# Attention scores as plain fp32 products in the two row halves of TensorE, without the split of q and k

## The reference

```python
# layer 0
xn = group_norm(x)                                   # 32 groups
q, k, v = split(qkv_w @ xn + qkv_b)                  # per head: 64 x 2304 each
x = proj_w @ (softmax(q^T k / 8) v) + proj_b + x
# layer 1: q and k come from x joined with a table of positions, v from x
q, k, v = [x, emb] @ Wq, [x, emb] @ Wk, x @ Wv
x = (softmax(q k^T / 8) v) @ Wout + bout + x
```

## Time and profile before

| | |
|---|---|
| median of 3 runs | 4401.74 us |
| the profiled execution | 4398.31 us |
| its span | 4396.5 us |
| attention of layer 0, layer 1 | about 420 to 2080 us, 2603 to 4265 us |
| TensorE, VectorE, ScalarE, GpSimd busy | 94%, 78%, 63%, 41% of the span |
| granted clock of TensorE, mean | 0.99 |

### The profile page before, as it was taken

How to read it: one execution, slowest core, us unless ns; L and a number is a source line. 1 busy time by engine, 2 the same in 40 slices (tenths; PEclk the granted TensorE clock), 3 DMA queues, 4 the chain that set the end, 5 groups by cost and what they waited for, 6 DMA issues and landing times. The chain is left out here.

```text
span 4396.5 us, 84946 instructions
## 1 busy us (share of the span) xinstructions
PE 4117.0 (94%) x29976; PEld 2458.3 (56%) x29976; DVE 3426.9 (78%) x3564; ACT 2790.3 (63%) x2981; POOL 1802.6 (41%) x584
## 2 busy tenths in 40 slices
PE   7998899999999999998999979999999999999989
PEld 4554555555555555554555545555555555555545
DVE  4222899999999999998433339999999999999972
ACT  1111788888888888886001027888888888888840
POOL 0000455555555555555100005555555555555540
PEclk9999999999999999999999999999999999999999
DMA  4334111212112111120444441212112111111216
GB/s 191 136 127 142 31 49 39 61 35 55 43 49 51 38 50 44 47 68 32 157 144 162 139 133 24 61 35 59 38 50 55 38 48 39 52 41 50 61 43 208
DMA packets 234733, 321.67 MB, mean 73 GB/s; under 512 B 12081, under 2 KB 221105, under 8 KB 233649
## 3 DMA queue, kind: packets, MB, share of 16 engines
q1 hardware_dynamic: 214512, 292.54, 23.0%
q10 hardware_dynamic: 20160, 28.32, 1.8%
HBM read 188.69 MB, written 132.12 MB: 73 GB/s over the span
## 5 line engine op out<-in xcount | busy, mean ns | idle before, releaser
L617 POOL TENSOR_TENSOR prob<-prob,mx 128x1344 f32<-128x1344 f32 x576 | 1781.6, 3093 | 2433.0 <-DVE two_tiles L894 1445.0
L772 ACT ACTIVATE prob<-psum_att 128x1152 f32<-128x1152 f32 x1152 | 1290.4, 1133 | 597.6 <-DVE run L874 336.4
L706 PE MATMUL psum_att<-qst,kst 128*128 128x384 f32 x6912 | 1420.2, 349 | 48.7 <-DMA kst<-qk_scratch 27.9
L785 ACT ACTIVATE prob<-prob 128x1152 f32<-128x1152 f32 x1152 | 1299.2, 1166 | 37.5 <-POOL prob L617 37.5
L706 PEld LDWEIGHTS psum_att<-qst,kst 128*128 128x128 f32 x6912 | 1177.1, 190 | 185.6 <-ACT prob L772 91.4
L719 PE MATMUL psum_att<-prob,vst 128*32 128x384 f32 x13824 | 1237.5, 491 | 34.6 <-ACT pvr L791 29.3
L617 DVE TENSOR_TENSOR prob<-prob,mx 128x960 f32<-128x960 f32 x576 | 974.1, 1691 | 173.0 <-ACT mx L779 173.0
L874 DVE TENSOR_TENSOR run<-psum_att,run 128x1152 f32<-128x1152 f32 x768 | 1004.3, 1347 | 13.0 <-PE psum_att L706 12.8
L719 PEld LDWEIGHTS psum_att<-prob,vst 128*32 128x32 f32 x13824 | 399.5, 109 | 625.1 <-issue 594.7
L894 DVE TENSOR_TENSOR two_tiles<-prob 128x768 f32<-128x768 f32 x576 | 565.9, 983 | 0.0
L314 PE MATMUL psum<-xc_l,wq 128*128 128x384 f32 x1536 | 504.3, 490 | 11.0 <-DVE hl_l L419 5.8
(11 more groups left out here) (59 smaller groups left out, 1906.7 us busy)
## 6 DMA issues: line engine op xcount, KB each, us to landing
qk_scratch<-hl_l SPq DMA_DIRECT2D x48, 1536.0 KB, 5.6
qst<-qk_scratch SPq DMA_DIRECT2D x192, 384.0 KB, 5.6
kst<-qk_scratch SPq DMA_DIRECT2D x192, 192.0 KB, 3.3
v_scratch<-vo_l SPq DMA_DIRECT2D x24, 768.0 KB, 3.5
vst<-v_scratch SPq DMA_DIRECT2D x96, 192.0 KB, 2.5
att_scratch<-ob ACTq DMA_DIRECT2D x96, 192.0 KB, 1.9
attc_l<-att_scratch SPq DMA_DIRECT2D x24, 768.0 KB, 5.5
x_sb<-in_x SPq DMA_DIRECT2D x8, 1152.0 KB, 14.1
```

The lines of the kernel that those rows point to most:

```text
L617: return engine.tensor_tensor(x, x, m, ALU.subtract)
L706: mm = nc.tensor.matmul(psum[:, 3 * e + k, 0:CH], kst[:, e, (3 * c + k) * P:(3 * c + k + 1) * P], qst[par][:, 2 * w + e, :], start=(w == 0 ...
L772: nc.scalar.activation(chunk_of(par, c, e), s_bank(e), ACT.Copy).then_inc(copied, 1)
L785: nc.scalar.activation(x, x, ACT.Exp, scale=SCALE).then_inc(exp_done, 1)
```

## The change

- `qkv_stage` makes no high and low part: ScalarE (layer 0, L360) or VectorE (layer 1, with the table) writes q and k once, in fp32. `qk_scratch` has one plane.
- A score tile is one fp32 product per head over 64 rows, head 0 in rows 0 to 63 and head 1 in rows 64 to 127 of TensorE, into two banks.
- A slot is one key tile for both heads (two banks, 128x768), three slots per chunk. `copy` and `maximum` work on slots: 18 and 16 per block, in place of 12 and 10 of 128x1152. The exponential is one of 128x2304 per chunk. All folds are one maximum of 128x768.
- The transposes of both heads stand together ahead of the chunk's scores. `turn_den` becomes three small products with a 128x2 matrix `heads`, which also drops the reduction L904. `reduce` and `norm` become three each, one per bank pair.
- SHIFT_DVE goes from 160 to 208. VectorE pairs before it shifts, and GpSimd waits for VectorE's shift of the same chunk instead of for a pair.
- q and k are loaded by one transfer per block, and one per chunk of keys.

```diff
-SHIFT_DVE = 160
+SHIFT_DVE = 208
...
-                        sp.dma_start(qkv["qk"].rearrange("m w p t -> p (m w) t")[:, half * MT:(half + 1) * MT, tokens(i)],
-                                     hl[half].rearrange("p m w t -> p (m w) t")).then_inc(stored, 16)
+                        sp.dma_start(qkv["qk"].rearrange("m p t -> p m t")[:, half * CT:(half + 1) * CT, tokens(i)],
+                                     qk[half][:, :, :]).then_inc(stored, 16)
...
-                            nc.vector.tensor_tensor(low, bufs["sum"][m % 2][:, :], high, ALU.subtract)\
-                                .then_inc(low_done, 1)
...
+                            nc.vector.tensor_tensor(qk[half][:, mt, :], qk_bank(m), emb_of(i, m), ALU.add)\
+                                .then_inc(qk_out, 1)
...
             def turn_den(t):
                 pe.wait_ge(den_copied, t + 1)
                 for r in range(3):
-                    mm = nc.tensor.transpose(spare_bank(0, r), den[:, r * P:(r + 1) * P], ident)
+                    mm = nc.tensor.matmul(psum[:, 5, CH + 2 * r:CH + 2 * r + 2], den[:, r * P:(r + 1) * P], heads,
+                                          start=True, stop=True)
...
+            def scores(t, par, c, k):
+                if c == 0 and k == 0:
+                    pe.wait_ge(q_in[par], 16 * (t // 2 + 1))
+                if k == 0:
+                    pe.wait_ge(k_in[c], 16 * (t // JB + 1))
+                for e in range(2):
+                    rows = slice(e * D, (e + 1) * D)
+                    mm = nc.tensor.matmul(psum[:, 2 * k + e, 0:CH], kst[rows, (3 * c + k) * P:(3 * c + k + 1) * P],
+                                          qst[par][rows, :], start=True, stop=True, tile_position=(e * D, 0))
                 mm.then_inc(scored, 1)
...
             def body(t, par):
                 for c in range(KC):
...
+                    spare_free(t, c)
+                    if c == TURN_AT and not before(t, 1) and live(t - 1):
+                        bank_free(t, c, 2)
+                        turn(t - 1)
+                    if c == BROADCAST_AT and not before(t, 1) and live(t - 1):
+                        bank_free(t, c, 2)
+                        broadcast_max(t - 1)
...
+                    if live(t):
+                        for k in range(3):
+                            bank_free(t, c, k)
+                            scores(t, par, c, k)
...
-                nc.scalar.activation(chunk_of(par, c, e), s_bank(e), ACT.Copy).then_inc(copied, 1)
+                nc.scalar.activation(prob[par][:, :, s, :], s_banks(k)[:, :, 0:CH], ACT.Copy).then_inc(copied, 1)
...
-                nc.vector.tensor_tensor(r[:, :, :], s_bank(e), other, ALU.max).then_inc(maxed, 1)
+                nc.vector.tensor_tensor(r[:, :, :], s_banks(s % 3)[:, :, 0:CH], other, ALU.max).then_inc(maxed, 1)
...
                         pool.wait_ge(copied, slot(t, 3 * c + 2))
-                        pool.wait_ge(paired, group(t, c))
+                        pool.wait_ge(dve_shifted, group(t, c))
                         shift_part(nc.gpsimd, par, c, SHIFT_DVE, CH).then_inc(pool_shifted, 1)
```

More of the change, by code:

```diff
@@ L6 @@
 F32 = mybir.dt.float32
-F32R = mybir.dt.float32r
 ALU = mybir.AluOpType
@@ L675, in turn @@
[L675 to L684 removed]
+                    pe.wait_ge(mx_ready, t)
@@ new lines, in spare_free, with turn @@
+                if c == DEN_TURN_AT + 1 and not before(t, 3) and live(t - 3):
+                    pe.wait_ge(inverted, t - 2)
+                if c == DEN_SPREAD_AT + 1 and not before(t, 3) and live(t - 3):
+                    pe.wait_ge(normed, 3 * (t - 2))
+            def turn(t):
+                pe.wait_ge(folded, t + 1)
+                for e in range(2):
+                    for r in range(3):
+                        mm = nc.tensor.transpose(psum[:, 2 * r + e, CH:512], fold[:, e, r * P:(r + 1) * P], ident)
+                mm.then_inc(turned, 1)
@@ L736, in body @@
                 for c in range(KC):
[L737 to L748 removed]
+                    spare_free(t, c)
[5 more added lines that the diff above has]
+                        broadcast_max(t - 1)
+                    if c == DEN_TURN_AT and not before(t, 3) and live(t - 3):
+                        bank_free(t, c, 2)
+                        turn_den(t - 3)
+                    if c == DEN_SPREAD_AT and not before(t, 3) and live(t - 3):
+                        bank_free(t, c, 2)
+                        spread_den(t - 3)
+                    if live(t):
+                        for k in range(3):
+                            bank_free(t, c, k)
+                            scores(t, par, c, k)
                     tv, pv, cv = behind(t, par, c, PV_LAG)
@@ L863, in maximum @@
-            def maximum(t, par, c, e):
-                r = run[e]
-                dve.wait_ge(scored, scored_count(slot(t, c, e)))
-                if c == 1:
-                    dve.wait_ge(copied, slot(t, 0, e))
+                    dve.wait_ge(broadcast, t)
+                nc.vector.tensor_reduce(mcol[:, :, r], s_banks(r)[:, :, CH:512], AX.X, ALU.max).then_inc(reduced, 1)
+            def maximum(t, par, s):
+                r = run[s % 2]
+                dve.wait_ge(scored, scored_count(slot(t, s)))
+                if s < 4:
+                    dve.wait_ge(copied, slot(t, s - 2))
@@ L884, in shift @@
-            def shift(t, par, c):
-                if c == 0:
-                    dve.wait_ge(mx_ready, unit(t, 1))
-                dve.wait_ge(copied, slot(t, c, 1))
-                shift_part(nc.vector, par, c, 0, SHIFT_DVE).then_inc(dve_shifted, 1)
+                    dve.wait_ge(turned, t)
+                nc.vector.tensor_tensor(fold[:, :, :], run[0][:, :, :], run[1][:, :, :], ALU.max).then_inc(folded, 1)
             def pair_tiles(t, par, c):
-                dve.wait_ge(exp_done, slot(t, c, 1))
+                dve.wait_ge(exp_done, group(t, c))
@@ L895, in pair_tiles, with shift @@
                                         prob[par][:, :, 3 * c + 1, :], ALU.add).then_inc(paired, 1)
+            def shift(t, par, c):
+                if c == 0:
+                    dve.wait_ge(mx_ready, t + 1)
+                dve.wait_ge(copied, slot(t, 3 * c + 2))
+                shift_part(nc.vector, par, c, 0, SHIFT_DVE).then_inc(dve_shifted, 1)
             def invert(t):
```

302 lines of the change are left out of this document (119 added, 183 removed).

## The result

The kernel after takes 4349.5 us (median of four runs, 4348.8 to 4350.6) against 4401.4 for the kernel before: a ratio of 0.9883, 95% interval 0.9866 to 0.9901. It is faster by 52 us where I forecast 131. The profiled execution has a span of 4347.7 us.

A forecast was written before the change was run, and what follows sets the result against it. TensorE and VectorE were both near their limit, so the chain between them set the block: 33.8 to 32.5 us over 96 blocks saves 125, the starts 6, 4398 to 4267 profiled, 4270 median; range 4185 to 4430.

The forecast's parts named there:

- maxima and fold of c=5 to 32.4. I take 32.5: End of the chain of a block: VectorE's fold done at 32.4 us, taken as 32.5 because some handoffs are missed.
- First tile to its reader, 0.90: Chain at c=1: broadcast and two tiling changes done at 6.3 us, first tile's maximum at 7.2.
- Chunk 2.06, tiling change 0.1: TensorE: a chunk's scores take 1.96 us, 2.06 with the change of tiling; a change costs about 0.1.
- Rival 3: Tiling changes cost up to 0.34 us for 0.1, eight on the chain: 34.1 a block, 4425 us; chance 0.07.
- `turn_den` 1.15: TensorE: three small fp32 products, six instructions at 0.19 us, 1.15 in all, +0.85 a block; alternatives 0.6 and 1.7.
- stays covered: ScalarE: 25 us a block and 1.5 of small work, below 33, so it does not set the pace.
- rival 1: TensorE's scores: row halves do not overlap, twelve rounds a chunk, 11.8 us more a block, 5360 us; chance 0.12.
- Rival 2: TensorE's scores: row halves overlap in part, seven rounds for six, 33.8 us a block, 4390 us; chance 0.08.
- The sums of work: Work per block after the change: TensorE 32.0 us, VectorE 29.9 us plus 0.6 behind GpSimd at c=0.
- VectorE idle ahead of every first maximum: Named sign that the forecast is wrong: VectorE waiting before the first maximum of every chunk.
- Outside the blocks: 3 us each start.: TensorE's two 14 us waits for the first k shrink by 3 us each, bounds 0 and 7.
- dropping it gives nothing more: `qkv_stage`: the split on ScalarE and VectorE lies under TensorE's products, so dropping it saves no further time.

The follow-up runs named there:

- e8: Kernel after with its new slots, order, shift split and `turn_den`, but before's fp32r products, high and low parts and transfers: 4353.3 us, ratio 0.9894.
- e12: e8 with the three edits of e7 and the exponential of c=3 put ahead of that chunk's copies: 4262.3 us, ratio 0.9688.
- e1: Kernel after with ScalarE's copy of `pvr` moved ahead of the exponential of c=3: 4335.5 us, ratio 0.9852.
- e7: Kernel after with e1's edit, the maxima copied before the last slot of c=1, and `turn_den` between second and third tile of c=2: 4294.3 us, ratio 0.9760.
- e4: Kernel after with a chunk's six score products issued as three of head 0, then three of head 1: 5078.9 us, a single run.
- e5: Kernel after with SHIFT_DVE back at 160, so GpSimd shifts 1344 elements again: 4359.6 us, ratio 0.9908.

## Why the prediction was right and wrong

**The step that failed** is "maxima and fold of c=5 to 32.4. I take 32.5": I walked one chain, and allowed 0.1 for all missed handoffs. The block is 33.56 (the mean of two neighbours). The 4349.5 lies inside the range that I gave, but that is luck: up there the range stood on a `turn_den` of 1.7 and dearer changes of tiling, and `turn_den` came out cheap. By its own milestones (us from the end of the fold, forecast and measured): scores 0.8 and 0.93; first maximum of c=1 7.2 and 7.70; maxima copied 11.35 and 12.05; first maximum of c=2 13.55 and 13.96; first normalization 18.7 and 19.37; first maximum of c=5 28.95 and 29.88; fold 32.4 and 33.56. It grows in small terms:

- *First tile to its reader, 0.90.* Measured 1.12 and 1.06 (1240.91 to 1242.03, 1247.23 to 1248.29) and 1.11 at c=3 (1252.59 to 1253.70). The 0.2 is paid at c=1 to c=3: 0.6 in all, the largest term. I had two rounds of 0.33 and 0.25 for the handoff. The first round of a chunk takes 0.42, and from the end of both rounds to the reader it is 0.3 to 0.4.
- *Chunk 2.06, tiling change 0.1.* Measured 2.13, and 0.14 to 0.18 for each change from transposes to row halves (by the lines of e8 and e12, which have no such change there). The Trainium skill ("TensorEngine Tiling (Array Packing)", Key Properties) only says that a change drains the engine; the drain is real and cost more than the 0.1 that the earlier trace rows gave for another pair of tilings. Rival 3 is thus half right: not 0.2 more on eight changes, but some 0.06 on four, and that sufficed, with the rest, to undo the form's gain.
- *`turn_den` 1.15.* Measured 0.73 to 0.76 with the change, which I had at 0.1 more: 0.5 too dear. Without this error the forecast would have been further off.
- *A wait not listed.* I let `weigh` go on without asking what stands ahead of `pvr`'s copy on ScalarE. The exponential of both halves in one instruction does (2.12 us); VectorE then stands 0.24 at c=5. ScalarE "stays covered" was right of its sum and wrong of its order. e1 shows 14 us for it.
- *Tails.* The third `reduce` is 0.22 late; three maxima and the fold 0.2 longer than priced.

e1 and e7 show that a part of this could be given back by order alone: with ScalarE's two copies moved and `turn_den` behind the second tile the block is 32.96, and with the exponential moved 32.88, near the 32.5 that I forecast for the order as it was.

**Right, and confirmed.** The row halves run side by side, in rounds of 0.32 (rival 1 falls; e4 shows what happens otherwise). Rival 2 falls too: the chunk has six rounds, 2.13, and not the 2.55 that I had estimated from four row tiles at 3.07 times in the Trainium skill ("TensorE: Matmul & The Clock Gate", Part 3); two row tiles on other banks cost the time of one. The sums of work: TensorE 32.0 against 32.2 busy, VectorE 29.9 and 0.6 behind GpSimd against 30.8. The first is in part luck, since `turn_den` was priced too high and chunks and changes of tiling too low. In the blocks no shift takes above 1.46, where the earlier trace rows had 3.32, and one pair, at c=0, is blocked: 1.18 for 0.95, so 0.23 where I had 0.6. The Trainium skill ("SBUF — State Buffer", SBUF: two separate sides) describes the shared pair as held for a whole instruction, and e5 agrees: the pair of 1.51 ends one free pair after GpSimd ends. VectorE's idle at the maxima copy, forecast 0.75, is 0.80. Of the signs that I named for being right, the chunk was near (2.13 for 2.06) and only the block of 32.5 was not there. But one sign of being wrong was nearly there, and it points at the step that failed: VectorE idle ahead of every first maximum. In the lines of after it waits for TensorE's first tile at c=1 (0.75), c=2 (0.45), c=3 (0.42) and c=5 (0.24).

**"Outside the blocks: 3 us each start."** Measured 34 us in all. The starts gave 4.8 and 5.1, inside their bounds of 0 to 7. I left out the fill and the drain of each layer, where no other block covers a stage: they gave 9.2 and 8.3 us. e8 has the same, so they come with the new layout; of the drain's 8.3, 5 go with the new shift split (e5). That the fill's part comes from slots of one key tile is likely but not shown alone, and the next three blocks took 1.6 us of it back. And "dropping it gives nothing more" failed: before, TensorE waited 3.59 us for the second image's statistics on VectorE, which made low parts between them; e8, which makes low parts too, has the same 3.59, and after does not wait. TensorE before and after at that place:

```profile
83.44 0.59 PE L81 MATMUL psum<-gn_mv,const_sb 128*128 128x4 f32 x2 [3.59 <-DVE gn_mv L74]
```

```profile
79.36 0.28 PE L78 MATMUL psum<-gn_mv,const_sb 128*128 128x4 f32 x2
```

The earlier trace rows shows this line at the start of the kernel, held for 19.07 us by the same releaser; I read the row for its length, not for its releaser. About half of the 6.9 us is that one wait. The two errors, 110 too much in the blocks and 28 too little at the edges, are the 82 us between the 4267 that I gave for the profiled execution and its 4349.5.

## What to carry to other kernels

When two engines are near full, cut the repeated block where the pace passes from one to the other, and price each part by what is late there: an edit that takes away one of two equally late things shows little or nothing alone. Two such edits, 15 us less and 13 us more by themselves, made part one 0.42 us shorter together, and with e1 the three gave 55 us where their sum was 16. An instruction made longer on a covered engine (one exponential for two) delays whatever is queued behind it, so read its order, not its share. And look at what lies outside the repeated block separately, the first and the last passes of a pipeline above all: here all of it gave more than twice what the 94 blocks did.

## What the runs showed of the hardware that I had not expected

- Two products of 64 rows each, fp32 with 384 columns, in the two halves of the rows and on different banks, start 6 to 7 ns apart and cost the time of one: a round of 0.32 us. The first round of a chunk takes 0.42. Given head by head instead, the same twelve instructions take 2.89 us for 2.13, with the first two and the last two uncovered, and a product of head 1 starts ahead of one of head 0 that stands before it in the queue, while the increments come in the queue's order (e4).
- In e4, and not in after, the granted clock falls from 1.00 to 0.5 again and again in the middle of attention, for 3.4 or 6.8 us about once in two blocks, with TensorE busy 70.2 of the 75 us before one such fall. A chunk then took 4.54 us for 2.89.
- A change from transposes on the whole array to products in row halves costs TensorE 0.14 to 0.18 us more than one to products on the whole array (0.78 against 0.64, 0.80 against 0.62). Six fp32 products with 64 rows gain only 0.15 over twelve fp32r ones with 128, so one change per chunk cancels the form.
- From the start of a two-instruction fp32 product of 384 columns to the start of its reader on VectorE it is 1.05 to 1.12 us, where its two rounds alone take 0.74.
